# A four-layer graph network on one core: layer 2's destination scores kept turned in SBUF instead of transferred by SyncE

## What is computed

```python
for h in range(W.shape[0]):
    Wh = x @ W[h]
    es = Wh @ a_src[h]
    ed = Wh @ a_dst[h]
    e = jax.nn.leaky_relu(es[src] + ed[dst], LRELU_ALPHA)
    att = _seg_softmax(e, dst, n)
    out = jax.ops.segment_sum(att[:, None] * Wh[src], dst, num_segments=n)
```

## Time and profile before

| what | us |
|---|---|
| median of 3 runs | 2941.07 (2940.23 to 2944.43) |
| span of the profiled execution | 3321.3 |
| the profiled execution's own time | not given |
| PE busy | 2643.0 (80%) |
| DVE busy | 1663.3 (50%) |
| POOL busy | 1410.3 (42%) |
| ACT busy | 980.3 (30%) |
| chain that ended last | PE 62%, DVE 10%, issue 9%, unknown 5% |
| DMA packets | 183897, 227.24 MB |

### The profile page before, as it was taken

The page is one execution under the profiler, slowest core; times in us unless marked ns, Lnnn a source line. Parts: engine busy times, 40 slices in busy tenths (PEclk is TensorE's granted clock), DMA queues, the critical chain, the costliest instruction groups (busy, mean ns, idle before and its releaser), DMA issues.

```text
span 3321.3 us, 56445 instructions
## 1 busy us (share of the span) xinstructions
PE 2643.0 (80%) x15058; PEld 1980.1 (60%) x15146; DVE 1663.3 (50%) x6677; ACT 980.3 (30%) x4757; POOL 1410.3 (42%) x1667
## 2 busy tenths in 40 slices
PE   2444545598448888889499998989699999999998
PEld 1444444455337787778367776767566666666665
DVE  4555555597334555554244545444854444444442
ACT  2444555465212333333123333333800000000000
POOL 3666666300156666661445656660232222222210
PEclk9999999999655555555695667677899999999999
DMA  2111111163233333331423333332610000000001
GB/s 77 44 44 45 44 45 44 44 227 114 79 82 91 89 92 92 91 89 46 106 70 83 90 84 90 89 89 59 231 59 18 17 18 18 18 17 18 17 28 42
DMA packets 183897, 227.24 MB, mean 68 GB/s; under 512 B 62447, under 2 KB 146488, under 8 KB 182808
## 3 DMA queue, kind: packets, MB, share of 16 engines
q0 software_dynamic: 50176, 131.74, 14.8%
q1 hardware_dynamic: 122654, 86.45, 8.3%
q10 hardware_dynamic: 10746, 5.37, 0.6%
HBM read 183.92 MB, written 39.48 MB: 67 GB/s over the span
## 4 chain that ended last, share of the span: by engine, by line
PE 62%; DVE 10%; issue 9%; another core or an unknown queue 5%; ACT 3%; ACTq 2%; DMA 2%; SPq 0%; DVEq 0%; POOL 0%; POOLq 0%
PE banks L2510 26%; PE banks L1538 7%; PE banks L1599 4%; PE banks L1596 3%; PE banks L1597 3%; PE banks L1602 2%; PE banks L748 2%; PE banks L1600 2%; DMA arena<-dst_flat 2%; PE banks L537 1%; PE banks L540 1%; DVE arena L524 1%; PE banks L1554 1%; PE banks L2521 1%
## 5 line engine op out<-in xcount | busy, mean ns | idle before, releaser
L2510 PE MATMUL banks<-arena 128*128 128x384 bf16 (+1 forms) x5475 | 879.8, 324 | 0.0
L2510 PEld LDWEIGHTS banks<-arena 128*128 128x128 bf16 x5475 | 535.7, 98 | 341.7
L222 POOL DMA_INDIRECT arena<-value_table,arena x392 | 396.4, 1011 | 487.2 <-DMA ed_table<-arena 267.0
L222 POOL DMA_INDIRECT arena<-gat_table,arena x392 | 389.7, 994 | 347.1 <-PE banks L1602 169.0
L222 POOL DMA_INDIRECT arena<-h_table,arena x392 | 371.8, 948 | 218.0 <-PE banks L540 90.9
L537 PE MATMUL banks<-arena 128*128 128x425 bf16 x392 | 201.8, 515 | 310.2 <-DVE arena L524 179.6
L2493 POOL TENSOR_TENSOR arena<-arena 128x128 f32<-128x128 f32 x225 | 103.3, 459 | 647.5 <-DVE arena L2567 638.2
L2561 DVE TENSOR_REDUCE arena<-banks 128x128 f32<-128x384 f32 x225 | 125.3, 557 | 364.3 <-PE banks L2510 356.7
L1538 PE MATMUL banks<-arena 128*128 128x512 bf16 (+1 forms) x902 | 279.3, 406 | 17.6 <-issue 15.3
L2551 ACT ACTIVATE arena<-arena 128x128 bf16<-128x128 f32 (+1 forms) x200 | 61.9, 309 | 732.4 <-DVE arena L2567 732.4
L1596 PE MATMUL banks<-arena 128*128 128x17 f32 x784 | 227.6, 371 | 43.3 <-issue 27.2
(11 more groups left out here) (282 smaller groups left out, 4601.6 us busy)
## 6 DMA issues: line engine op xcount, KB each, us to landing
adj_rows<-arena SPq DMA_DIRECT2D x1, 20000.0 KB, 54.6
arena<-adj_rows SPq DMA_DIRECT2D x2, 7200.0 KB, 22.0
arena<-h_rows SPq DMA_DIRECT2D x225, 64.0 KB, 1.8
arena<-ed_table SPq DMA_DIRECT2D x784, 0.5 KB
arena<-h_table,arena POOLq DMA_INDIRECT x392
arena<-value_table,arena POOLq DMA_INDIRECT x392
arena<-gat_table,arena POOLq DMA_INDIRECT x392
arena<-adj_rows SPq DMA_DIRECT2D x2, 1600.0 KB, 6.2
```

Source lines behind the costliest of these rows:

```text
L222: return e.indirect_dma_start(into, None, table, bass.IndirectOffsetOnAxis(ap=index.bitcast(U32), axis=0))
L2510: x = e.matmul(acc[:, 0:w], C[:, sb, db * P:(db + 1) * P], old[:, sb, 0:w], start=(sb == 0), stop=(sb == LAST))
```

## The change

Destination scores no longer go through DRAM. They stand turned, 8 heads on partitions 32 to 39 and 3200 nodes along the free dimension, in an array `EDT`. `layer1_tables` and `layer2_mid` each compute them with a second product whose stationary operand is the 8 score vectors, and ScalarE or VectorE copies it to `EDT`. In layer 2's edges ScalarE loads the window starts of the next batch into registers and copies eight slices of 16 columns (`ed_windows`); TensorE turns the [8 x 128] result into the second PSUM bank (`turn_windows`), beside the turned logits, and VectorE's `expand` reads it there. The destination lists are written in setup as 16-bit integers (`dst_short`) and loaded once, in 16 transfers behind the layer 1 tables, for all 49 batches and both passes; SyncE has nothing to do in layer 2's edges. In `layer2_mid` the scores use one PSUM bank in place of two, so each group waits for the copy of the one before.

```diff
@@ -162,6 +162,7 @@
+        dst_short = dram("dst_short", [1, NC * P + 2], I16)
@@ -192,6 +193,8 @@
+        EDT = at(keep_end, [NP])[32:32 + H]
+        DST = at(keep_end, [NBATCH, P + 2], I16)[64:64 + BC * H]
@@ -226,6 +229,9 @@
+        short_made = sem("short_made")
+        dst_landed = [sem("dst_landed0"), sem("dst_landed1")]
+        DST_PARTS = [(0, 7), (7, NBATCH - 7)]
@@ -292,7 +298,8 @@
-            gtile = s0.get([2], I32)
+            gtile, gshort = s0.get([2], I32), s0.get([2], I16)
+            short = s0.get([T, P], I16)
@@ -341,6 +349,12 @@
+                flat = dst_short[0:1, :]
+                e.wait_ge(short_made, 1)
+                e.dma_start(flat[:, 1:1 + (T - 1) * P * P].rearrange("o (t p e) -> (o p) t e", p=P, e=P), short[:, 0:T - 1, :]).then_inc(flat_stored, 16)
+                e.dma_start(flat[:, 1 + (T - 1) * P * P:1 + NC * P].rearrange("o (p e) -> (o p) e", e=P), short[0:nr, T - 1, :]).then_inc(flat_stored, 16)
+                e.dma_start(flat[:, 0:1], gshort[0:1, 0:1]).then_inc(flat_stored, 16)
+                e.dma_start(flat[:, NC * P + 1:NC * P + 2], gshort[0:1, 0:1]).then_inc(flat_stored, 16)
@@ -378,6 +392,7 @@
+                e.tensor_copy(short, raw["d"]).then_inc(short_made, 1)
@@ -976,7 +991,7 @@
-            ROW = 2 * D + 2 * H
+            ROW = 2 * D + H
@@ -991,7 +1006,7 @@
-            stored, tabled = node_stored[0].use(16 * NG), tables_stored.use(32 * NG)
+            stored, tabled = node_stored[0].use(16 * NG), tables_stored.use(16 * NG)
@@ -1011,8 +1026,11 @@
-                    e.dma_start(blocks(value_table)[:, b0:b0 + n, :], T0[:, b0:b0 + n, 0:2 * D + H]).then_inc(tabled.sem, 16)
-                    e.dma_start(blocks(ed_table[0])[:, b0:b0 + n, :], T0[:, b0:b0 + n, 2 * D + H:]).then_inc(tabled.sem, 16)
+                    e.dma_start(blocks(value_table)[:, b0:b0 + n, :], T0[:, b0:b0 + n, :]).then_inc(tabled.sem, 16)
+                for (b0, n), landed_in in zip(DST_PARTS, dst_landed):
+                    for j in range(BC):
+                        ap = bass.AP(tensor=dst_short.tensor, offset=(b0 * BC + j) * P, ap=[[0, H], [BC * P, n], [1, P + 2]])
+                        e.dma_start(DST[j * H:(j + 1) * H, b0:b0 + n, :], ap).then_inc(landed_in, 16)
@@ -1050,7 +1068,9 @@
-                        e.matmul(banks[:, 4 + b % 2, 0:ROW], H2t[g % 2][:, (b - b0) * P:(b - b0 + 1) * P], early.WT, start=True, stop=True).then_inc(n1_table, 1)
+                        h2 = H2t[g % 2][:, (b - b0) * P:(b - b0 + 1) * P]
+                        e.matmul(banks[:, 4 + b % 2, 0:ROW], h2, early.WT[:, 0:ROW], start=True, stop=True)
+                        e.matmul(banks[32:32 + H, 4 + b % 2, 3 * P:4 * P], early.WT[:, ROW:ROW + H], h2, start=True, stop=True).then_inc(n1_table, 1)
@@ -1099,7 +1119,8 @@
-                        e.activation(T0[:, b, :], banks[:, 4 + b % 2, 0:ROW], ACT.Copy).then_inc(n1_rows, 1)
+                        e.activation(T0[:, b, :], banks[:, 4 + b % 2, 0:ROW], ACT.Copy)
+                        e.activation(EDT[:, b * P:(b + 1) * P], banks[32:32 + H, 4 + b % 2, 3 * P:4 * P], ACT.Copy).then_inc(n1_rows, 1)
@@ -1308,13 +1328,13 @@
-            R4, R3, RS, RE, RO = 4, 3, 7, 3, 5
+            R4, R3, RS, RO = 4, 3, 7, 5
-            EDR = [space.get([H]) for _ in range(RE)]
+            EDW = [space.get([P])[32:32 + H] for _ in range(2)]
+            ed_rows = banks[:, 2, P:P + H]
-            DLI = [space.get([P + 2], I32, 64) for _ in range(2)]
@@ -1366,21 +1385,6 @@
-            def sp(e):
-                begin(e)
-                first = Windows(e, FI, f"e2w_{i}")
-                for b in range(NBATCH):
-                    if b >= RE:
-                        e.wait_ge(e2_bd, nb0 + b - RE + 1)
-                    first.load(b * BC)
-                    for j in range(BC):
-                        e.dma_start(EDR[b % RE][j * WIN:(j + 1) * WIN, :], first.rows(ed_table[i], b * BC + j)).then_inc(of_windows[b % RE], 16)
-                    ap = bass.AP(tensor=dst_flat.tensor, offset=b * BC * P, ap=[[P, BC], [0, H], [1, P + 2]])
-                    if b >= 2:
-                        e.wait_ge(e2_dstf, nb0 + b - 1)
-                    e.dma_start(DLI[b % 2], ap).then_inc(e2_dst[b % 2], 16)
-                first.free()
@@ -1395,10 +1399,12 @@
-                    e.wait_ge(e2_dst[b % 2], 16 * (before(2, b % 2) + b // 2 + 1))
+                    for (b0, _), landed_in in zip(DST_PARTS, dst_landed):
+                        if i == 0 and b == b0:
+                            e.wait_ge(landed_in, 16 * BC)
-                    e.tensor_copy(DLF[b % 2], DLI[b % 2]).then_inc(e2_dstf, 1)
+                    e.tensor_copy(DLF[b % 2], DST[:, b, :]).then_inc(e2_dstf, 1)
@@ -1415,10 +1421,10 @@
-                    e.wait_ge(of_windows[b % RE], windows0[b % RE] + 16 * BC * (b // RE + 1))
+                    e.wait_ge(e2_edt, nb0 + b + 1)
-                    e.tensor_tensor(BD[b % 2], EDR[b % RE].unsqueeze(1).broadcast_to([P, BC, H]),
+                    e.tensor_tensor(BD[b % 2], ed_rows.unsqueeze(1).broadcast_to([P, BC, H]),
@@ -1546,6 +1552,12 @@
+                def turn_windows(b):
+                    e.wait_ge(e2_edw, nb0 + b + 1)
+                    if b:
+                        e.wait_ge(e2_ztc, nb0 + b)
+                    e.transpose(ed_rows, EDW[b % 2], ident[32:32 + H, 32:32 + H]).then_inc(e2_edt, 1)
@@ -1610,6 +1622,8 @@
+                        if q == 0 and p < NBATCH:
+                            turn_windows(p)
@@ -1624,7 +1638,16 @@
-                first = Windows(e, FI, f"e2_{i}")
+                first, ahead = Windows(e, FI, f"e2_{i}"), Windows(e, FI, f"e2w_{i}")
+                scored(e)
+                def ed_windows(b):
+                    ahead.load(b * BC)
+                    if b >= 2:
+                        e.wait_ge(e2_edt, nb0 + b - 1)
+                    for j in range(BC):
+                        x = e.activation(EDW[b % 2][:, j * WIN:(j + 1) * WIN], ahead.of(EDT, b * BC + j), ACT.Copy)
+                    x.then_inc(e2_edw, 1)
@@ -1685,6 +1708,7 @@
+                ed_windows(0)
@@ -1699,6 +1723,8 @@
+                        if q == 7 and p < NBATCH - 1:
+                            ed_windows(p + 1)
@@ -1827,17 +1854,17 @@
-            V, ES, SV = space.get([2 * H]), space.get([NB, 2 * H]), space.get([NB, H + 1])
+            V, ES, SV = space.get([2 * H]), space.get([NB, H]), space.get([NB, H + 1])
-            stored = tables_stored.use(16 * (2 * NG + 2))
+            stored = tables_stored.use(16 * (2 * NG + 1))
-                e.wait_ge(stored.sem, stored.at(16 * (2 * NG + 2)))
+                e.wait_ge(stored.sem, stored.at(16 * (2 * NG + 1)))
@@ -1854,8 +1881,7 @@
-                e.dma_start(blocks(gat1_table)[:, :, D:D + H], ES[:, :, 0:H]).then_inc(stored.sem, 16)
-                e.dma_start(blocks(ed_table[1]), ES[:, :, H:2 * H]).then_inc(stored.sem, 16)
+                e.dma_start(blocks(gat1_table)[:, :, D:D + H], ES).then_inc(stored.sem, 16)
@@ -1889,11 +1915,11 @@
-                    if g >= 2:
-                        e.wait_ge(added.sem, added.at(g - 1))
+                    if g:
+                        e.wait_ge(added.sem, added.at(g))
-                        x = e.matmul(banks[:, k, q * 2 * H:(q + 1) * 2 * H], HT[k][:, q * P:(q + 1) * P], V, start=True, stop=True)
-                    x.then_inc(scored.sem, 1)
+                        e.matmul(banks[:, 0, q * H:(q + 1) * H], HT[k][:, q * P:(q + 1) * P], V[:, 0:H], start=True, stop=True)
+                    e.matmul(banks[32:32 + H, 1, 0:n * P], V[:, H:2 * H], HT[k][:, 0:n * P], start=True, stop=True).then_inc(scored.sem, 1)
@@ -1971,7 +1997,8 @@
-                    e.tensor_copy(ES[:, b0:b0 + n, :], banks[:, g % 2, 0:n * 2 * H].rearrange("p (b s) -> p b s", s=2 * H)).then_inc(added.sem, 1)
+                    e.tensor_copy(ES[:, b0:b0 + n, :], banks[:, 0, 0:n * H].rearrange("p (b s) -> p b s", s=H))
+                    e.tensor_copy(EDT[:, b0 * P:(b0 + n) * P], banks[32:32 + H, 1, 0:n * P]).then_inc(added.sem, 1)
@@ -3026,8 +3053,8 @@
-            return [layer0_edges(), sums, n1, Stage(sp=wt.sp), layer2_edges(0, n1.done), m0, Stage(act=wt.act, dve=wt.dve, pe=wt.pe),
-                    layer2_edges(1, m0.done), m1, diffusion(m1.done)]
+            return [layer0_edges(), sums, n1, Stage(sp=wt.sp), layer2_edges(0, n1.done, lambda e: e.wait_ge(n1_rows, NB)), m0, Stage(act=wt.act, dve=wt.dve, pe=wt.pe),
+                    layer2_edges(1, m0.done, scored), m1, diffusion(m1.done)]
```

More of the change, by code:

```diff
@@ L317, in pool @@
                 e.memset(norm.X[:, NB - 1, :], 0.0)
+                e.memset(gshort, GUARD)
                 e.memset(gtile, GUARD).then_inc(fills_made, 1)
@@ L425, in setup_done @@
             e.wait_ge(setup_made, 1)
-            e.wait_ge(flat_stored, 192)
+            e.wait_ge(flat_stored, 256)
         def layer_norm_of():
@@ L1001, in done @@
                 e.wait_ge(stored.sem, stored.at(16 * NG))
```

(11 more changed lines are left out.)

## The result

The changed kernel takes 2985.23 us (median of 4 runs, 2976.32 to 3028.43), the kernel before 2942.75 us in the same session. The ratio is 1.0118, with a 95% interval of 1.0082 to 1.0155: slower by 1.2%, some 35 us.

What follows compares the result with a forecast made beforehand. It took TensorE to bound layer 2's first pass and the diffusion, with most SyncE stalls absent from timed runs. Terms 10 + 5 + 15 + 7 = 37, less 4, gave +33 on 2941.1: 2974 us, range 2880 to 3010.

Steps and rivals of the forecast that it cites:

- The stalls in the first profile are not in the timed runs: Most stalls around SyncE's transfers held to be the profiler's own; 380.2 us lie between profiled span and median.
- my first sign: In the changed kernel's profile the two 48 us stretches are gone and the span falls by far more than the median.
- Layer 1 tables, +10 (bounds +5 and +11): Layer 1 tables: each of 25 blocks gains a narrow score product, 10.8 us less 0.7, so +10 us.
- Middle, +5 (bounds +3 and +16): Middle of layer 2: added score product and copy, one bank for all groups, mostly hidden; +5 us.
- Layer 2, TensorE, first pass +15: Layer 2's first pass, bound by TensorE: one added transpose a batch, 12 us, and a new wait, 3 us; +15.
- Second pass +7: Layer 2's second pass: same transpose and wait, but higher clock half the time and more TensorE slack; +7 us.
- Rival C: Layer 2: TensorE has slack in both passes, only tables and middle show; 2952 us, or 2941; chance 0.10.
- ScalarE 0: Layer 2: a register load and eight copies a batch, 1.9 us, fall in ScalarE's idle time; 0 us.
- Rival B: Layer 2: ScalarE becomes the bound, adding 98 times 0.5 to 1.0 us; 3020 to 3070 us; chance 0.13.
- Removed transfers 0: Layer 2: removing 784 score and 98 list transfers of SyncE gains 0 us, bounds 0 and -68.
- Rival A: Layer 2: the stalls are real in the timed runs; fully 2726 us, with the starts alone 2906; chance 0.27.
- Less 4 for the stores: The two score tables no longer stored: some 4 us taken off the sum.

Runs made afterwards that it cites:

- first profile: The kernel before, in its original profiled execution, no edit: span 3321.3 us, where the median of the runs was 2941.1 us.
- second profile of before: The kernel before, unchanged, profiled again: span 2939.8 us in an execution of 2941.63 us; median 2948.79 us, ratio 1.0018.
- full width: Changed kernel with the eight-column stationary side of the score products zero-padded to 128 columns, in tables and middle: 2982.60 us, 1.0095 of the kernel before.
- cheaper scores: Changed kernel with one turned-score product and copy per group in the tables, two banks and ScalarE copying in the middle: 2970.20 us, 1.0070 of the kernel before.
- experiment 4, no copies: Changed kernel with ScalarE copying one slice of turned scores a batch instead of eight, from the third batch on: 2985.90 us, 1.0163 of the kernel before.
- experiment 3, lists once: Kernel before plus only the destination lists stored as 16-bit numbers and loaded once; score transfers stay: 2948.55 us, ratio 1.0022.
- Narrow at zero: Changed kernel with the eight-row score products sent to PSUM partitions 0 to 7 instead of 32 to 39: 2985.32 us, 1.0156 of the kernel before.
- scores turned alone: Kernel before plus only the making of turned scores in tables and middle, which are not read: 2975.02 us, ratio 1.0107.

## Why the prediction was right, and where its working was not

The forecast was +33 us to 2974, range 2880 to 3010; measured +42 by medians of one session, +35 by the ratio. The sign holds, for the reason given. The size holds in part by luck: the two stages were put 12 us too low, and the two passes 17 us too high beside the same pair of executions.

*The stalls in the first profile are not in the timed runs:* right, and the one step on which the sign hung. The timed runs' spans are 1.7 us under their times (2974.6 and 2976.32), and so is the second profile of before. But I called them "the profiler's own", around SyncE's transfers, and they were one execution's: every other profile here, with SyncE's transfers or without, is free of them. So my first sign, a span that falls far more than the median, would have come with no change at all and showed nothing of the change. The rule of a fixed gap of about 6.2 us from the Trainium skill ("Runtime: NRT & Kernel Launch", The ~15µs preamble/postamble breakdown), by which the profile's total is the longer one, agrees with neither: here the span is the shorter by 1.7 to 1.8 us, and once 380.2 above the median.

*Layer 1 tables, +10 (bounds +5 and +11):* this step failed. It was +17 (15 to 18 by the execution). I priced the added product alone, and took the 128-column products of line 1036 for it, whose loads are of full width. Its own part is right (0.40 us a block); the loads it leaves bare, 0.39 us at half clock, were not in the sum, nor in its bound. In the changed kernel's tables the loader's waits of this kind add up to 21.8 us (14.9 before narrow loads, 6.9 before wide ones); with the full width there are none.

*Middle, +5 (bounds +3 and +16):* this step failed too. It was +10, and for another reason than the tables. The score products' rows, before (second profile, 1335 to 1377 us) and changed (1358 to 1410 us):

```profile
L1895 PE MATMUL banks<-arena 128*128 128x16 f32 x50 | 7.3, 280 | 0.0
```
```profile
L1922 PE MATMUL banks<-arena 128*8 128x512 f32 (+1 forms) x14 | 7.6, 631 | 0.0
...
L1921 PE MATMUL banks<-arena 128*128 128x8 f32 x50 | 7.3, 272 | 2.6 <-DVE arena L2001 2.6
...
L2001 DVE COPY arena<-banks 8x512 f32<-8x512 f32 (+1 forms) x7 | 4.4, 628 | 0.1
```

The products over eight moving columns take as long as those over sixteen did, and the turned ones come on top with 7.6 us, less than the 12 that I had. I took most of that to be hidden, with only the last two groups in the open. It isn't: TensorE's busy time grows from 33.5 to 40.9 us, and its wait for VectorE's copy out of the one bank adds 2.6, together 10.0. The copies cost what was said, 4.4 us; the two banks give back about that wait (cheaper scores, 2.3).

*Layer 2, TensorE, first pass +15:* the turning costs 10 us (12 said), the wait for line 1645's copy (now 1668) 1.4 us (3 said). Its own row, both passes:

```profile
L1559 PE MATMUL banks<-arena x98: 222/271/271, 801.5 to 1919.5; 8*128 8x8 f32 x98
its engine sat idle before it (us, times) until:
  issue: 25.0, 53
  ACT arena L1649: 4.3, 1
  ACT arena L1668: 1.4, 3
```

The forecast's +15 reads as +4 beside the one traced execution of before, and as 9 beside the passes without turning (555.0 and 546.0). *Second pass +7:* +1 in this pair, mostly filled by gathers, but within the variation of the pass. Rival C was wrong of the first pass; of the second it isn't decided.

*ScalarE 0:* right; a batch's eight copies in the changed kernel's timeline:

```profile
1100.40 0.96 ACT L1649 ACTIVATE arena<-arena 8x16 f32 x8 [0.34 <-issue]
```

They take 0.96 us, 0.12 each, and with the register load's gap 1.3 us (1.9 said), and without seven of eight the pass doesn't change. Rival B falls with experiment 4. The Trainium skill's copy ("ScalarE: Activation LUTs", What ACT_TABLE_LOAD costs), 0.11 us by my estimate, agrees with that pace, and my 0.17 from a single record did not. *Removed transfers 0:* experiment 3 agrees for the lists. For the scores the paces do: 10.49 us a batch with all transfers, with those of the scores alone and with none. *Rival A:* 2726 to 2906 us; falls. *Less 4 for the stores:* not seen; VectorE waits 5.3 us for value_table after, and 4.0 for ed_table before. So 10 + 5 + 15 + 7 - 4 became 17 + 10 + 4 + 1 + 2: two parts too small, two too large, and the sums 33 and 34 agree by luck.

## What to carry to other kernels

When a profiled span is far from the timed median, take a second profile before anything is explained by the first; a stage that has none of the suspected work and is slow too already says so. Price a small product by what it does to its neighbours: in the tables a stationary side of 8 columns between full-width ones kept both loads bare, and cost as much again as the product. Padding them to full width or grouping them took 3 to 9 us off that stage; in the middle the padding gave nothing, so look at the loader's waits first. What is added to an engine is surely paid in the pass which that engine bounds: the same instruction cost 10 us in the first pass, and in the second none that could be told from a variation of 18. And compare a pace with twins of the same code: one execution of before would have made 10 us look like 4.

## What the runs showed of the hardware that was not expected

Zero-padding the stationary side from 8 to 128 columns made a pair of products faster, 1.31 against 1.70 us at 1.2 GHz.

Pass 2 runs at a mixture of both clock levels that differs between executions of one code. Narrow at zero and lists once, whose pass 2 are alike in work but for the turning:

```profile
1404.00:1940.00 536.00, 506.38 (x3544) 382.71 (x3607) 323.22 (x1584) 254.56 (x1712) 387.23 (x389) 0.95 0.37 100
```
```profile
1378.00:1927.00 549.00, 532.65 (x3557) 401.67 (x3555) 323.07 (x1583) 204.87 (x1324) 384.11 (x391) 0.87 0.38 99
```

536 us at a granted 0.95, 549 at 0.87: 13 us, as much as most effects here. The clock isn't all of it: at 0.89 the pass took 538.6 us in scores turned alone, 544.3 in before and 553.7 in no copies. What decides when the clock falls in this pass stays open, and with it why the changed kernel spreads more (2964 to 3004 us in its second session) than the kernel before (2936 to 2949 beside it).
